# Attention values weighed in three fp16 passes from the second batch on, and the relu's fp16 half cast by GpSimd

## The reference

```python
h = einsum('bhid,oi,od->bho', x, weighted_sum, weight)        # mixing
h = h + attention(layernorm(h))     # 16 heads of 16, rotary, q and k of unit length
#   attn = softmax(q @ k.T * HD**-0.5);  out = attn @ v;  out @ out_w.T + out_b
h = h + mlp(layernorm(h))           # 8 experts of 1024, all computed:
#   sum over e of gate_e * (relu(x @ W1_e + b1_e) @ W2_e + b2_e), gate_e 0 where sigmoid <= 0.5
```

## Time and profile before

| | |
|---|---|
| runs | 2010.56 us median of 3 (2005.82 to 2010.73) |
| the profiled execution | 2008.53 us |
| its span, first to last instruction | 2006.6 us |
| mean granted TensorE clock | 0.975 |
| TensorE busy | 1907.4 us, 95% |
| ScalarE busy | 1143.0 us, 57% |
| VectorE busy | 776.4 us, 39% |
| GpSimd busy | 676.7 us, 34% |
| chain that ended last | TensorE 78%, VectorE 8%, issue 6% |

### The profile page before, as it was taken

One profiled execution on the slowest core, in us unless ns is written; L12 is line 12 of the kernel. 1 busy time (PEld: TensorE's weight loads), 2 busy tenths in 40 slices (PEclk: granted clock), 3 DMA queues, 4 the chain that ended last, 5 costly groups with the idle time before them and its releaser, 6 DMA issues.

```text
span 2006.6 us, 33214 instructions
## 1 busy us (share of the span) xinstructions
PE 1907.4 (95%) x13152; PEld 1210.5 (60%) x13152; DVE 776.4 (39%) x1636; ACT 1143.0 (57%) x1969; POOL 676.7 (34%) x570
## 2 busy tenths in 40 slices
PE   5679898899999999999999999999999999999999
PEld 4246543576547764577646775467645776466666
DVE  6656933538103470145502372034800455022000
ACT  2654676544774467644765447754576447654444
POOL 1102422335223343333423353233433334233443
PEclk8779999999999999999999999999999999999999
DMA  4013232332112311231212221133211322113221
GB/s 156 31 57 113 104 138 84 126 138 84 64 64 106 115 64 64 79 125 63 83 64 105 97 84 64 64 106 97 83 64 64 124 77 85 64 64 116 101 89 53
DMA packets 40442, 176.64 MB, mean 88 GB/s; under 512 B 4056, under 2 KB 17120, under 8 KB 23904
## 3 DMA queue, kind: packets, MB, share of 16 engines
q1 hardware_dynamic: 40288, 174.52, 24.8%
HBM read 153.54 MB, written 20.97 MB: 87 GB/s over the span
## 4 chain that ended last, share of the span: by engine, by line
PE 78%; DVE 8%; issue 6%; ACT 1%; POOL 1%; POOLq 0%; DVEq 0%; ACTq 0%
PE bank_h L850 28%; PE bank_f L869 10%; PE bank_f L871 10%; PE bank_f L872 10%; PE bank_o L779 5%; PE bank_s L767 3%; PE bank_s L683 2%; PE bank_s L685 2%; PE bank_s L684 2%; PE bank_s L752 1%; DVE qk L972 1%; DVE tmp_b L967 1%; DVE y L890 1%; POOL hl L540 1%; PE bank_s L833 1%
## 5 line engine op out<-in xcount | busy, mean ns | idle before, releaser
L540 POOL TENSOR_TENSOR hl<-h,hh 128x512 f16<-128x512 f32 x512 | 608.2, 1188 | 1131.8 <-ACT hh L660 724.9
L850 PE MATMUL bank_h<-x,w1s 128*128 128x512 f16 x3072 | 754.8, 383 | 9.0 <-ACT hh L660 8.6
L657 ACT ACTIVATE h<-bank_h,b1s 128x512 f32<-128x512 f32 x512 | 353.6, 691 | 453.3 <-PE bank_h L850 438.3
L869 PE MATMUL bank_f<-w2s,hh 128*128 128x256 f16 x2048 | 562.3, 275 | 2.1 <-DVE acc L1073 1.6
L871 PE MATMUL bank_f<-w2s,hh 128*128 128x256 f16 x2048 | 560.5, 274 | 0.0
L872 PE MATMUL bank_f<-w2s,hl 128*128 128x256 f16 x2048 | 560.4, 274 | 0.0
L850 PEld LDWEIGHTS bank_h<-x,w1s 128*128 128x128 f16 x3072 | 288.2, 99 | 333.9 <-issue 43.5
L660 ACT ACTIVATE hh<-bank_h,b1s 128x512 f16<-128x512 f32 x512 | 352.6, 689 | 0.0
L627 ACT ACTIVATE probs<-bank_s 128x512 f32<-128x512 f32 x480 | 262.4, 604 | 154.6 <-PE bank_s L767 154.2
L869 PEld LDWEIGHTS bank_f<-w2s,hh 128*128 128x128 f16 x2048 | 201.9, 99 | 112.5 <-issue 43.0
L1073 DVE SCALAR_TENSOR_TENSOR acc<-bank_f,gw,acc 128x256 f32<-128x256 f32 x256 | 106.1, 477 | 364.0 <-PE bank_f L872 363.9
(11 more groups left out here) (134 smaller groups left out, 1736.0 us busy)
## 6 DMA issues: line engine op xcount, KB each, us to landing
w1s<-w_parts SPq DMA_DIRECT2D x56, 1024.0 KB, 4.8
w2s<-w_parts SPq DMA_DIRECT2D x56, 1024.0 KB, 4.8
xraw<-in_x_t_dram SPq DMA_DIRECT2D x32, 512.0 KB, 4.8
raw<-in_w_dram SPq DMA_DIRECT2D x16, 1024.0 KB, 6.7
w_parts<-w1s SPq DMA_DIRECT2D x8, 1024.0 KB, 8.8
w_parts<-w2s SPq DMA_DIRECT2D x8, 1024.0 KB, 10.7
out_dram<-acc SPq DMA_DIRECT2D x16, 256.0 KB, 6.1
raw<-in_qkv_w_t_dram SPq DMA_DIRECT2D x1, 768.0 KB, 7.2
```

Of the source, the lines that this page charges most:

```text
L540: pool.tensor_tensor(hl[n % HBUFS][:], h32[n % 2][:], hh[n % HBUFS][:], ALU.subtract)\
L657: act.activation(h32[n % 2][:], bank_h[n % 2][:, :], ACT.Relu, bias=b1s[:, e, m:m + 1]).then_inc(h_hi.sem, 1)
L850: last = pe.matmul(bank_h[n % 2][:, :], w[:, wp, k, m * P:(m + 1) * P], x16s[fb % 2][:, xp, k, :], start=(k == 0 and wp + xp == 0), stop=( ...
L869: pe.matmul(o, high, w[:, 0, m, :], start=(m == 0 and t % 2 == 0), stop=False, skip_group_check=True)
```

## The change

From the second batch on the values and the exps are weighed as fp16 halves.

- Exps: each pair of heads is written to two neighbouring banks, `score_banks`, and read by two ScalarE instructions of 128x1024, one to fp32 (in the space of `qk`) and one to fp16 (the high half, in the space of `probs`). VectorE subtracts the high half for the low one in a new step, `halves`. The score matmuls of pair n wait for both exps of pair n-1.
- Values: VectorE adds the bias into a scratch tile, copies to the fp16 high half, and subtracts for the low half. `weigh` is twelve fp16 matmuls: high by high, low by high, high by low.
- The value weights and bias are scaled by a power of two once, and the output weights by its inverse (`scale_values`, in `projections`). The power comes from a maximum across partitions, with partition_all_reduce.
- The first batch keeps the fp32 weighing, with its values in the space of `w2s[1]`.
- MLP: ScalarE makes only the fp32 relu. GpSimd casts it to fp16, waits for that, and subtracts.

```diff
+        steps += [(first + PACE * n, "scores", n), (first + PACE * (n + 0.8), "halves", n)]
# GpSimd
                 if stage == "f1":
-                    wait(pool, h_hi, fb, 2 * (n + 1))
+                    wait(pool, h_out, fb, n + 1)
                     wait(pool, f2_done, fb, n - HBUFS + 1)
+                    pool.tensor_copy(hh[n % HBUFS][:], h32[n % 2][:]).then_inc(h_hi.sem, 1)
+                    wait(pool, h_hi, fb, n + 1)
                     pool.tensor_tensor(hl[n % HBUFS][:], h32[n % 2][:], hh[n % HBUFS][:], ALU.subtract)\
                         .then_inc(h_lo.sem, 1)
+                elif stage == "projections":
+                    pool.wait_ge(v_max, 1)
+                    pool.partition_all_reduce(vmxr[:], vmx[:], P, bass.bass_isa.ReduceOp.max).then_inc(v_max_all, 1)
...
+            pool.memset(v_first[:, :, :, 1, :], 1.0)
+            pool.memset(v1[:, 0, :, :, 1, :], 1.0)
+            pool.memset(v1[:, 1, :, :, 1, :], 0.0).then_inc(pool_consts, 1)
# ScalarE
                 elif stage == "projections":
-                    act.wait_ge(proj_in, 32)
+                    act.wait_ge(v_scaled, 1)
...
+                    wait(act, scored, ab, 2 * n + 2)
+                    wait(act, qk_unit, ab, TT)
+                    wait(act, halved, ab - 1, n - 1)
+                    act.activation(exps[n % 2], score_banks(n, fb is None)[:, :, :], ACT.Exp, scale=SCORE_SCALE)\
+                       .then_inc(exped.sem, 1)
                     if half == 0:
                         wait(act, weighed, ab, u - 1)
+                    act.activation(halves[u % 2][:, 0, 2 * half:2 * half + 2, :], score_banks(n, fb is None)[:, :, :],
+                                   ACT.Exp, scale=SCORE_SCALE).then_inc(exped.sem, 1)
...
                     act.activation(h32[n % 2][:], bank_h[n % 2][:, :], ACT.Relu,
-                                   bias=b1s[:, e, m:m + 1]).then_inc(h_hi.sem, 1)
-                    wait(act, f2_done, fb, n - HBUFS + 1)
-                    act.activation(hh[n % HBUFS][:], bank_h[n % 2][:, :], ACT.Relu,
-                                   bias=b1s[:, e, m:m + 1]).then_inc(h_hi.sem, 1)
+                                   bias=b1s[:, e, m:m + 1]).then_inc(h_out.sem, 1)
# TensorE
+                    if not first_batch(fb):
+                        wait(pe, exped, ab, 2 * n)
                     for j in range(2):
+                        if first_batch(fb):
+                            wait(pe, exped, ab, 2 * n + j - 3)
...
+                        wait(pe, halved, ab - 1, 2 * (n + 1))
...
+                    for vp, pp in ((0, 0), (1, 0), (0, 1)):
+                        for j in range(4):
+                            h = 4 * g + j
+                            last = pe.matmul(bank_o[32 * j:32 * j + 32, :],
+                                             v1[:, vp, tile, h, :, :].rearrange("p s d -> p (s d)"),
+                                             halves[n % 2][:, pp, j, :], start=(tile == 0 and vp + pp == 0),
+                                             stop=(tile == TT - 1 and pp == 1), skip_group_check=True)
# VectorE
+                    values = tmp_b[:, 0:D]
+                    wait(dve, summed, ab, n)
+                    half_v.link(dve, dve.tensor_tensor(values, at_v[:, 0:D], qkvb[:, 2 * D:QKV], ALU.add))
+                    values = values.rearrange("p (h d) -> p h d", d=HD)
+                    half_v.link(dve, dve.tensor_copy(v1[:, 0, n, :, 0, :], values))
+                    dve.tensor_tensor(v1[:, 1, n, :, 0, :], values, v1[:, 0, n, :, 0, :], ALU.subtract)\
                        .then_inc(qkv_out.sem, 1)
...
+                elif stage == "halves":
+                    u, half = divmod(n, 2)
+                    high, low = (halves[u % 2][:, part, 2 * half:2 * half + 2, :] for part in range(2))
+                    wait(dve, exped, ab, 2 * n + 2)
+                    dve.tensor_tensor(low, exps[n % 2], high, ALU.subtract).then_inc(halved.sem, 1)
...
+            def scale_values():
...
+                dve.tensor_reduce(vmx[:], w_v, AX.X, ALU.max, apply_absolute_value=True).then_inc(v_max, 1)
+                dve.wait_ge(consts_in, 16 * 9)
+                dve.tensor_reduce(vbound[:, 1:2], b_v, AX.X, ALU.max, apply_absolute_value=True)
+                dve.wait_ge(v_max_all, 1)
...
+                dve.tensor_scalar(w_v, w_v, vscl[:, 0:1], None, ALU.mult)
+                dve.tensor_scalar(raw_out, raw_out, vscl[:, 1:2], None, ALU.mult)
+                dve.tensor_scalar(b_v, b_v, vscl[:, 0:1], None, ALU.mult).then_inc(v_scaled, 1)
+                dve.wait_ge(v_scaled, 1)
```

More of the change, by code:

```diff
@@ L74, in attention_order @@
     for n in range(2 * UNITS):
-        steps.append((first + PACE * n, "scores", n))
+        steps += [(first + PACE * n, "scores", n), (first + PACE * (n + 0.8), "halves", n)]
     for u in range(UNITS):
@@ L139, in bodies @@
     first = [("mix_weights", 0)]
-    for step in attention_order(alone=True):
+    for step in [s for s in attention_order(alone=True) if s[1] != "halves"]:
         first += [step[1:]] + between.get(step[1:], [])
@@ L247, in build @@
         kt = sb("kt", [P, HEADS // 2, TOKENS], F16)
-        v1 = sb("v1", [P, TT, HEADS, 2, HD])
+        v1 = sb("v1", [P, 2, TT, HEADS, 2, HD], F16)
+        v_first = w2s[1][:].rearrange("p s k d -> p (s k d)").bitcast(F32)\
+            .rearrange("p (t h s d) -> p t h s d", t=TT, h=HEADS, s=2)
         probs = [sb(f"probs{i}", [P, 4, TOKENS]) for i in range(2)]
+        halves = [p[:].rearrange("p j t -> p (j t)").bitcast(F16).rearrange("p (s j t) -> p s j t", s=2, j=4)
+                  for p in probs]
+        exps = [qk[:, 2 * i:2 * i + 2, :] for i in range(2)]
         xh = sb("xh", [P, XK, P], F32R)
@@ L285, in build @@
         scl = sb("scl", [P, 2])
-        bank_s = [bank(f"bank_s{i}") for i in range(2)]
+        vmx = sb("vmx", [P, DK])
+        vmxr = sb("vmxr", [P, DK])
+        vbound = sb("vbound", [P, 2])
+        vscl = sb("vscl", [P, 2])
+        both_s = two_banks("bank_s")
+        bank_s = [both_s[:, i, :] for i in range(2)]
         bank_m = bank("bank_m")
         bank_o = bank("bank_o")
-        bank_h = [bank(f"bank_h{i}") for i in range(2)]
+        both_h = two_banks("bank_h")
+        bank_h = [both_h[:, i, :] for i in range(2)]
         bank_f = [bank(f"bank_f{i}") for i in range(2)]
@@ L370, in build, with score_banks, first_batch @@
         block = ctx.enter_context(nc.Block())
-        def score_bank(n, alone):
-            return ([bank_s[0], bank_s[1], bank_h[0], bank_h[1]] if alone else bank_s)[n % (4 if alone else 2)]
+        def score_banks(n, alone):
+            return both_h if alone and n % 2 else both_s
+        def first_batch(fb):
+            return fb is None
         def qkv_banks(t, alone):
@@ L664, in steps @@
                     act.wait_ge(scales, e + 1)
+                    if e == 1 and p == PIECES // 2:
+                        wait(act, weighed, 0, UNITS)
                     if e >= 2 and p == 0:
@@ L770, in steps @@
                     g, tile = divmod(n, TT)
-                    wait(pe, exped, ab, 4 * (n + 1))
+                    if first_batch(fb):
+                        wait(pe, exped, ab, 4 * (n + 1))
+                    else:
+                        wait(pe, halved, ab - 1, 2 * (n + 1))
                     if n == 0:
@@ L844, in steps @@
                         wait(pe, w1_in[e % 2], fb - 1, 16 * (e // 2 + 1))
-                    wait(pe, h_hi, fb, 2 * (n - 1))
+                    wait(pe, h_out, fb, n - 1)
                     w = w1s[e % 2]
@@ L908, in steps @@
                         att_v.start(ab)
+                        if not first_batch(fb):
+                            half_v.start(ab - 1)
                     wait(dve, x_in[n % 2], ab, 16 * (n // 2 + 1))
@@ L960, in steps @@
                     row = qk[:, n, :]
-                    wait(dve, qkv_out, ab, 2 * n + 1)
+                    wait(dve, qkv_out, ab, 2 * n + 2)
                     pairs = row.rearrange("p (h f two) -> p h f two", f=HD // 2, two=2)
```

62 lines of the change are left out of this document (46 added, 16 removed).

## The result

| | before | after |
|---|---|---|
| runs, median (least to most) | 2010.64 us of 4 (2005.82 to 2016.69) | 2089.64 us of 4 (2088.35 to 2090.67) |
| after over before | | 1.0389, 95% interval 1.0371 to 1.0407 |
| the profiled execution, its span | 2008.53, 2006.6 us | 2089.87, 2088.1 us |
| mean granted TensorE clock | 0.975 | 0.971 |

The account below looks back on a forecast made before the run. TensorE, busy 95% of the span, was taken as the bound, with the exp loop stalling its score matmuls. 2008.5 + 37 (merged batches) + 5 (values) + 8.4 (start) + 12 (second batch) = 2070.9, stated as 2070 us, range 2036 to 2105.

Parts of the forecast that it names:

- The loop in the score stretch: Merged batches: score pairs wait for both exps, start to start 2.50 us; net +6.1 us a batch, +37 over six.
- the four intervals with a relu ahead: Merged score stretches: a relu before the exps in four short intervals costs another 0.2 to 0.4 us each.
- The fp16 pass: Weigh units: three fp16 rounds take 0.78 us instead of 1.00, saving 25 us on PE, bounds 11 to 39.
- Rival (c): Weigh units: the fp16 passes save nothing, a unit stays at 1.00 us; total 2095 us; chance 0.04.
- The start: First batch: value scaling with partition_all_reduce delays the DVE chain, +8.4 us; +3 if GpSimd's switch is free.
- Second batch: Scores beside weight preparation: the loop's 6.1 us plus exposed ScalarE weight casts, taken as +12 us, between 3 and 22.
- VectorE between the stretches: Qkv tiles: two more DVE instructions each, bounds 0 and 3.3 us, taken as 0.8 a merged batch, +5.
- The cast: MLP: GpSimd's 128x512 cast takes 0.85 us, with subtraction 2.0 against 2.68 per chunk, so hidden; taken as 0.
- the rule: GpSimd and VectorE share SBUF interfaces, contending when VectorE has two SBUF inputs; at worst 3.3 us once more.
- Rival (b): MLP: GpSimd becomes the bound at a cast over 1.4 us; at 1.6 us total 2090; chance 0.07.
- Rival (d): Slack elsewhere repays: start and second batch cost nothing, 1.9 us of idle comes back; total 2037; chance 0.06.
- (a): Score stretch: two exps take 1.2 us or less, so no interval stalls; total 1992 us; chance 0.03.

Follow-up runs that it names:

- the one with the add: Changed kernel, but VectorE adds the values' fp16 high half straight from PSUM instead of copying it from the scratch tile: 2094.32 us, ratio 1.0421.

## Why the prediction was right, and where its sizes were off

- **The loop in the score stretch: right, in size too.** Forecast 2.50 us, measured 2.45; wide exps 1.03 to 1.05, measured 1.025 and 1.022; the four intervals with a relu ahead came out at 2.67, 2.86, 2.68 and 2.85. The stretch was to be 79.0 + 9.6 and is 88.21; leaving the second exp out gives 79.14. What the prediction got right is the view it chose: ScalarE's load in the stretch, 72.4 of 88.3 us, is not the bound; the loop through one pair of banks is. (Where ScalarE has both relus too, the load shows: 93.73.)
- **The fp16 pass: right.** One weigh unit takes 0.76 us (0.78 forecast), and TensorE's busy time fell by 21.4, where 25 was said. Part of the difference is the lower clock (0.971 against 0.975). Rival (c) is out.
- **The start: right.** +9.0 in the trace, 9.4 by the kernel without scaling, about 8 by the first score over all traces, 8.4 forecast. The subtraction that was to start at 25.8 starts at 26.4. The 4.2 us more in the rest of the first batch had no term; TensorE waits there 6.3 us for VectorE's chunk sums, which the rows of before don't show as a wait in that place.
- **Second batch: the term that was most mis-sized, 22.9 for 12, or 27 with the stretch ahead of it.** It was built from the loop and from ScalarE's weight casts. TensorE's idle time in the stretch is 30.9 us, 11.6 before, and 20.6 of it is `weigh` behind VectorE. The step that failed is "The 32 subtractions of halves [...] lie where DVE was busy 7 of 83 us and the weigh unit comes two score steps later: nothing". That is true of merged batches, where the wait was not seen; but in the second batch the same subtractions stand in VectorE's list behind a step that waits for GpSimd. The prediction priced where VectorE has room and did not ask behind which waits the new step is queued. The row for it was there: 5.85 us ahead of a partition_all_reduce, which it used for the start only. The kernel with one exp parts the 22.9: 11.7 us go with the second exp, and 11.2 stay, with 19.7 us of waits for the halves. The one move of the scales that was tried did not get it back, since GpSimd's idle time around each maximum then came through ScalarE.
- **VectorE between the stretches: 11.9 for 5.** The term counted two more instructions for each value tile, within bounds of 0 to 3.3 a batch; measured 2.4 a batch, within them, and I took 0.8. The kernel with the weighing alone has 1.8 without any cast, so the counted cause is most of it and was priced too low; the cast adds 0.6 in the mean. A between has VectorE at 90.5 us for 79.1: 5.5 of the 11.4 are there with the weighing alone (84.6), 5.2 with the cast alone (84.3).
- **The cast: 0 was wrong.** It took 0.80 us in the mean (0.85 forecast) and TensorE hardly waits for it. But alone it makes the kernel 18 us slower, through VectorE and the clock. I had named the rule, put its worst at one more 3.3 us a batch, and left it out of the sum. That sentence gave GpSimd 45 us more a batch; 64 casts at the 0.85 forecast make 54, and 53 was measured. The parts don't add: 18 alone, 106 for the weighing alone, 79 for both.
- **The range held**, from its upper half. Rival (b), 2090, gives the time by the wrong mechanism: GpSimd is busy 145.2 of the last 231.0 us, and the last MLP is 0.89 us shorter than before. (Its condition, a cast over 1.4 us, is 1.49 by its own sum, 2.68 - 1.19.) Who looks at the total alone would take it for confirmed. Rival (d) would have had start and second batch at nothing, (a) an interval below 2.44; neither is seen.

## What to carry over

For a step that is added, ask two things besides its duration and the engine's free time: how many buffers its input holds busy, since the loop through them (here 2.45 us for a pair of banks) stalls an engine long before any load is full; and behind which waits it is queued on its own engine, stretch by stretch. Work that is moved to GpSimd is not hidden by being off the critical path if VectorE is near that path: price it by VectorE's busy time for the same instructions. And an idle place of 2.6 to 3.2 us on TensorE can cost 1.4 to 1.7 us more in the clock behind it, in some places and not in others; count it as a chance, not as a sum. It isn't always lost either: the one of after's five betweens that kept full clock is the longest, 155.75 us, with one more wait of 2.5 on TensorE.

## What was not expected of the hardware

The cast of 128x512 takes 0.60 us at least and 0.61 in the median, yet 0.80 in the mean and 2.84 at most. The prediction's 0.6 fits the shortest. By the Trainium skill's figures ("GPSIMD Engine Reference", the per-element model: about 1.03 cycles an element at 1.2 GHz) the body alone is an estimated 0.44 us; the page has no price for what remains. What disturbs works both ways: VectorE operations often end together with a GpSimd operation (131 of the 239 that are over 0.25 us longer than their shortest, in the kernel with the cast alone, end within 0.15 us of one). One such pair in after:

```profile
1002.95 2.35 POOL L589 TENSOR_TENSOR resid<-resid,outb 128x1024 f32<-128x1024 f32 x1
...
1003.08 2.27 DVE L942 TENSOR_SCALAR y<-y 128x64 int32<-128x64 int32 x1
```

The VectorE operation has one input of 64 elements and takes 0.20 us at its shortest; here it ends at 1005.35, 0.05 after GpSimd's. That reads as held until the other was done, not slowed. Such cases are the likely source of the 5.2 us by which VectorE's same 169 instructions are longer with the cast; they were not added up. The clock was the other surprise. After's TensorE, idle until 1016.4 for a sum on VectorE:

```profile
1014.00:1016.00 2.00, 0.00 (x0) 0.00 (x0) 2.00 (x5) 0.51 (x1) 1.92 (x2) 1.00 0.93 369
1016.00:1018.00 2.00, 1.61 (x8) 1.17 (x9) 2.00 (x5) 1.21 (x3) 1.19 (x2) 0.54 0.30 123
1018.00:1020.00 2.00, 2.00 (x10) 1.08 (x8) 1.93 (x5) 0.00 (x0) 1.92 (x2) 0.61 0.00 0
1020.00:1022.00 2.00, 2.00 (x26) 1.60 (x24) 1.86 (x5) 1.26 (x3) 1.14 (x2) 1.00 0.00 0
```

After 2.60 us of idle time the granted clock is at its lower level for some 3 us. The same 2.61 us in the same place before 1259.54, the 3.23 us before 1705.11 in the kernel with the cast alone and the 2.68 us before 1024.74 in the one with the add were followed by full clock. So the length of the idle time doesn't decide it here, and what does is open. In merged batches of the kernel before, at 1.00 throughout, this never came up.
